# Two reorderings in the streaming part of a graph kernel: word numbers before the row sums on TensorE, raw scores before the copies of turned rows on ScalarE

## The reference

```python
h = relu(layernorm(x))
H = h @ W.T + b; s = H @ a_s; r = H @ a_r
e = leaky_relu(A * s + A * r.T, 0.2)
att = softmax(where(A > 0, e, -9e15), axis=1)
x = x + att @ H                          # layer 0: attention over the neighbours
h = relu(layernorm(x)) @ weight
out = relu(adj @ h + bias)
x = x + max over the neighbours of out   # layer 1: sum, then graph max-pool
```

## Time and profile before

| | us |
|---|---|
| median of 3 runs | 2826.6 |
| lowest and highest | 2820.92, 2831.66 |
| the profiled execution | 2835.18 |
| its span in the trace | 2826.0 |
| the stretch in which steps 18 to 76 run | about 280 to 1430 |

### The profile page before, as it was taken

The page is one execution under the profiler, slowest core; times in us unless marked ns, Lnnn a source line. Parts: engine busy times, 40 slices in busy tenths (PEclk is TensorE's granted clock), DMA queues, the critical chain, the costliest instruction groups (busy, mean ns, idle before and its releaser), DMA issues.

```text
span 2826.0 us, 19035 instructions
## 1 busy us (share of the span) xinstructions
PE 968.4 (34%) x4534; PEld 535.7 (19%) x4534; DVE 1438.5 (51%) x3301; ACT 456.3 (16%) x1519; POOL 1562.0 (55%) x1616
## 2 busy tenths in 40 slices
PE   3664156525245536423539996600000000000000
PEld 1431133213122213323514432300000000000000
DVE  6888677855334525443265543547656345222222
ACT  1631145302123214433410000000000000000000
POOL 0102755444664645576363564677766755677776
PEclk8987577767677768666759997855555555555555
DMA  9999668788567879632441221152232111222121
GB/s 351 410 381 375 189 239 291 283 224 321 194 241 244 297 261 387 212 79 70 120 97 40 75 61 48 51 132 59 67 56 43 52 42 40 48 57 54 49 47 41
DMA packets 155983, 447.42 MB, mean 158 GB/s; under 512 B 34557, under 2 KB 81459, under 8 KB 122970
## 3 DMA queue, kind: packets, MB, share of 16 engines
q1 hardware_dynamic: 80506, 311.94, 29.2%
q0 software_dynamic: 53184, 114.44, 16.9%
q10 hardware_dynamic: 22176, 19.77, 2.3%
HBM read 408.06 MB, written 37.95 MB: 158 GB/s over the span
## 4 chain that ended last, share of the span: by engine, by line
another core or an unknown queue 20%; POOL 18%; PE 16%; issue 15%; DVE 11%; DMA 6%; DVEq 6%; ACT 4%; SPq 2%; ACTq 1%; POOLq 0%
POOL ring L661 16%; PE psV L1093 9%; DMA a_buf<-in_adj 5%; PE psV L920 3%; DVE squares L1330 2%; SPq L390 2%; ACT ring L764 2%; POOL out L667 1%; PE psH L976 1%; DVE a_buf L1495 1%; DVEq L1499 1%; DVE words L1221 1%; DVE words L1212 1%; DVEq L1215 1%
## 5 line engine op out<-in xcount | busy, mean ns | idle before, releaser
L589 POOL DMA_INDIRECT ring<-h_table,srec x518 | 506.5, 978 | 304.0 <-issue 170.3
L661 POOL DMA_INDIRECT ring<-p_table,srec x545 | 529.8, 972 | 200.3 <-issue 166.9
L920 PE MATMUL psV<-a_buf,bit_ident 128*128 128x512 bf16 x1024 | 318.4, 476 | 245.7 <-DMA a_buf<-in_adj 173.8
L1330 DVE TENSOR_REDUCE squares<-ring 128x128 f32<-128x640 f32 (+15 forms) x99 | 178.0, 1798 | 333.4 <-DMA ring<-p_table,srec 301.9
L976 PE MATMUL psH<-ring,ident 128*128 128x128 f32 x1036 | 159.3, 316 | 205.9 <-remote 93.2
L624 POOL DMA_INDIRECT ring<-y_table,srec x198 | 191.8, 969 | 62.4 <-issue 61.8
L1093 PE MATMUL psV<-rec_all,a_buf 128*128 128x512 bf16 x888 | 202.0, 385 | 26.0 <-issue 25.9
L1103 PE MATMUL psH<-ones_row,flag_col 128*1 128x1 f32 x2 | 0.2, 163 | 589.7 <-DVEq L1556 589.7
L920 PEld LDWEIGHTS psV<-a_buf,bit_ident 128*128 128x128 bf16 x1024 | 115.5, 115 | 432.3 <-issue 296.0
L976 PEld LDWEIGHTS psH<-ring,ident 128*128 128x128 f32 x1036 | 149.6, 228 | 220.2 <-issue 205.9
L1314 DVE SCALAR_TENSOR_TENSOR e_sc<-e_sc 128x6 f32<-128x6 f32 (+19 forms) x63 | 10.7, 170 | 259.1 <-ACT e_sc L748 245.0
(11 more groups left out here) (228 smaller groups left out, 2055.5 us busy)
## 6 DMA issues: line engine op xcount, KB each, us to landing
a_buf<-in_adj SPq DMA_DIRECT2D x256, 1024.0 KB
ring<-p_table,srec POOLq DMA_INDIRECT x545
ring<-h_table,srec POOLq DMA_INDIRECT x518
trec<-records ACTq DMA_DIRECT2D x63, 128.5 KB
packed<-wbuf ACTq DMA_DIRECT2D x28, 256.0 KB
a_buf<-packed SPq DMA_DIRECT2D x7, 1024.0 KB
h_table<-stage POOLq DMA_DIRECT2D x16, 258.0 KB, 7.6
a_buf<-r_row SPq DMA_DIRECT2D x1, 4096.0 KB
```

What stands on the lines that cost most here:

```text
L589: pool.indirect_dma_start(ring[:, A_AT[q] + j, :], None, h_table, bass.IndirectOffsetOnAxis(srec_u[g][:, i, LIST + j:LIST + j + 1], 0)).th ...
L661: pool.indirect_dma_start(ring[:, C_AT[n] + j, 0:D], None, p_table, bass.IndirectOffsetOnAxis(slot, 0)).then_inc(s_rows[n % BUFS], 16)
L920: last = pe.matmul(psV[n % 2][:, h * BANK:(h + 1) * BANK].rearrange("p (g n) -> p g n", n=P), bit_ident[:, k, :], rows[:, :, k, :], start= ...
L1330: dve.tensor_reduce(to, ring[:, at:at + n, 0:D].rearrange("p s d -> p d s"), AX.X, op)
```

## The change

On ACT, `raw_scores` of a step moves from behind the record loads to a place ahead of `tile_copies`. On PE, `number_words(n+1)` moves from behind `turn_rows` to directly behind `pack(n+1)`. Nothing is added or removed.

```diff
@@ scalar engine, step n @@
                 if 1 <= n <= 8:
                     normalize(2 * n - 2)
                     normalize(2 * n - 1)
+                for q in AT_STEP[n]:
+                    raw_scores(q)
                 if n in TURNS:
                     tile_copies(n)
                 if n in DENSE_STEP:
@@
                 for q in AT_STEP[n + 1] if n < LAST else []:
                     load_record(q)
-                for q in AT_STEP[n]:
-                    raw_scores(q)
                 for q in AT_STEP[n]:
                     exponents(q)
@@ tensor engine, step n @@
                 if n + 1 < T:
                     pack(n + 1)
+                if n + 1 < T - 1:
+                    number_words(n + 1)
                 for q in AT_STEP[n - 1]:
                     sum_slots(q)
                 if n in TURNS:
                     turn_rows(n)
-                if n + 1 < T - 1:
-                    number_words(n + 1)
```

## The result

The changed kernel takes 2816.84 us (median of 8 runs, 2811.45 to 2820.77) against 2826.4 us for the kernel before (8 runs, 2820.92 to 2832.97): ratio 0.9957, 95% interval 0.9945 to 0.9970. The forecast was 2816.6 us. A second comparison gave 0.9942 (0.9919 to 0.9965), 2819.56 against 2834.88 us.

A forecast was written before the change was run, and what follows sets the result against it. PE's signals, held to the end of gather runs, were taken to bound steps 18 to 76. Terms -3.0, -4.4, -2.6 and 0 gave -10 us, from 2826.6 to 2816.6; own range 2811 to 2824, full range 2799 to 2836.

The forecast's parts named there:

- Late signals: Steps 18 to 76: engines that wait for PE late in a run of gathers wait to the run's end.
- rival C: ACT itself stands still, so raw scores delay each turn by 0.40 us a tile: +10 us, 2837; chance 0.16.
- Numbers, 0: Word numbers directly behind the pack gain 0; in dense steps, if not hidden, they cost up to 3 us.
- T: The moment PE's signals arrive; copy, scatter and next gathers form a loop from it, whose length the change leaves.
- Group 1, -3.0: Step 19: raw scores no longer stand behind `keep_words`, so scores and POOL's next gather come 3 us earlier.
- Group 2, -4.4: End of group 2: the last extraction comes at 897.4 instead of 901.89, so POOL's start at 921.94 gains 4.4 us.
- Group 3, -2.6: End of group 3: DVE scores near 1184.1 instead of 1186.66, and the scatter at 1195.99 gains 2.6 us.
- The T cycle of steps 55 to 62 stays: Group 3: the loop from PE's signals to the next keeps its length; +0.6 at 55 and 56, given back at 61.
- Steps 64 to 76, 0: Raw scores cost +2.6 us in steps 70 to 72, about -2.6 in 73 to 75: sum 0, ends -3 and +3.
- A: Only the turn's signal is late, so DVE isn't held at the close and runs ahead: -25 us, 2802; chance 0.24.
- B: The gain is absorbed by PE's longer dense steps and another wait in group 2: -2 to -4 us, 2823; chance 0.15.
- D: The change does nothing, DVE being busy whenever raw scores are ready; counted inside the forecast and the absorbed-gain rival.

The follow-up runs named there:

- e9: The changed kernel plus two useless activations on ACT, ahead of its wait for the turn: ratio 0.9937 to the kernel before.
- e8: The changed kernel, with POOL waiting ahead of every fourth gather until its last one has landed: ratio 1.0458 to the kernel before.
- e5: The kernel before, unchanged, profiled a second time: record scatters of groups 1 to 3 at 518.9, 926.0 and 1192.0 us.
- e7: The changed kernel, with the numbers left behind the turn where the next tile's packed words are kept: ratio 0.9922 to the kernel before.
- e12: The kernel before, with raw scores moved only in steps 64 and later, signals held: ratio 0.9964 to the kernel before.
- e11: The kernel before, with only the raw scores moved, in every step, signals held: ratio 0.9921 to the kernel before.
- e10: The changed kernel plus two useless activations on ACT, behind the wait for the turn and ahead of the copies: ratio 0.9956 to the kernel before.
- e1: The kernel before, with only the raw scores moved, in every step, measured where no signals were held: ratio 0.9982 to the kernel before.
- e3: The kernel before, with raw scores moved only in steps 64 and later, measured where no signals were held: ratio 0.9975 to the kernel before.

## Why the prediction was right, and where it wasn't

**Late signals (right, and too narrow).** All that hung on "PE's signals arrive at the end of a run" was seen: DVE and ACT released together (896.18, 896.21), ACT working in the hold (e9), the hold gone with the gapless run (e8). It has exceptions in the long runs. In the changed kernel one copy comes at 827.75, 16.8 us into a run of 25 gathers (811 to 842), for a turn that ended at 799.77. And the extraction of step 52, which started at 1020.87 in the kernel before, 6.6 us after POOL's last instruction, starts in the middle of a run (974 to 1008) in the changed one:

```profile
998.03 1.23 DVE L1212 MAX8 words<-psV 128x8 f32<-128x1024 f32 x1 [23.01 <-remote]
```

Nor is the prediction's border, 5 us into the run, sharp: all turns later than that were held, but so was one that ended 3.6 us into its run (copy at 1140.75, 9.4 us late). And it isn't only signals. Late in a long run PE and DVE get single instructions, with nothing to wait for, 1.4 us or a multiple of it apart. In e5:

```profile
356.03 0.37 PE L976 MATMUL psH<-ring,ident 128*128 128x128 f32 x1 [2.52 <-issue]
...
358.83 0.37 PE L977 MATMUL psH<-trec,ident 128*128 128x128 f32 x1 [2.43 <-issue]
...
361.63 0.37 PE L977 MATMUL psH<-trec,ident 128*128 128x128 f32 x1 [2.42 <-issue]
```

```profile
354.68 0.57 DVE L1237 SCALAR_TENSOR_TENSOR node<-node,label 128x320 f32<-128x320 f32 x1 [2.31 <-issue]
...
357.47 0.49 DVE L1240 MAX8 rec_all<-node 128x8 f32<-128x320 f32 x1 [2.21 <-issue]
...
361.67 0.50 DVE L1245 MAX8 rec_all<-node 128x8 f32<-128x320 f32 x1 [2.24 <-issue]
```

ACT is not spared in the first long run (280 to 360). In the kernel before:

```profile
335.41 0.40 ACT L764 ACTIVATE ring<-ring,prob 128x128 f32<-128x128 f32 x1 [0.98 <-issue]
336.80 0.40 ACT L767 ACTIVATE trec<-trec,prob 128x128 f32<-128x128 f32 x1 [0.99 <-issue]
338.19 1.02 ACT L721 ACTIVATE wbuf<-psV 128x1024 bf16<-128x1024 f32 x1 [1.00 <-issue]
```

So an engine that is itself slowed does occur, as rival C had it, but not at the copies that the forecast rests on. What makes these steps of 1.4 us the traces don't show; code that arrives late, which the prediction left open, is not excluded for them.

**Numbers, 0: mis-sized.** T in steps 21, 23 and 25 became PE's, as said: the copies at 404.27, 445.36 and 479.98 come 0.03, 1.15 and 0.03 us behind the turn's end. But the price, 3 to 4 us from step 20 to step 26, was not hidden, and no gain by the early numbers is seen anywhere. It doesn't show at the end of group 1 because the raw scores gained as much in the same steps (113.9 and 114.0 us in the kernel before, 109.9 in e7; 115.1 in e12 and 110.6 in e11, of one comparison), which the forecast had at nothing behind step 19. Two terms that were both put at nothing cancel.

**Group 1, -3.0.** Measured -3.5 (mean of two executions each). In the changed kernel all of it is step 19, as said: the extraction of step 20 starts 3.3 us earlier, and the lead stays to the end of the group (3.7 at the extraction of step 26).

**Group 2, -4.4.** The sum to here was -7.4; measured -7.2 on the means, -5.0 on the first pair. The right sum has a wrong composition. The term itself held: DVE's distance from the last T before the last extraction fell from 5.35 (4.60 in the second trace) to 0.7 us. That group 1's 3.0 would add to it was the failed step: e7, e9 and e10 show the run of gathers up to 856 swallowing such shifts. The rest of the -7.2 is T itself, at 896.5 and 901.0 in the two executions of before and 896.2 and 896.0 in the changed ones: one late execution of the kernel before, and so luck in the mean.

**Group 3, -2.6: mis-sized, measured -7.5 for its stretch.** The forecast's own term is not in it: from the extraction of step 62 to the scatter the kernel before takes 29.1 and 24.3 us and the changed one 26.2 twice, so -2.9 on the first pair and -0.5 on the means. Some 3.3 us come at step 52, where the first execution of the kernel before had its extraction held to 1020.87; the second took 120.9 us from step 46 to step 53, nearly what the changed kernel does (120.1, 120.2). That part is scatter. The remaining 3.9 us are the change's. "The T cycle of steps 55 to 62 stays" was the failed step. It stays from step 57 on. In steps 55 and 56 no hold covers the turn: PE packs late (in the kernel before its matmuls at 1072.92 waited 5.14 us for a tile's load), and sums and turn follow. There DVE's distance counts in full. Step 56 before, then changed:

```profile
1082.42 0.27 PE L998 MATMUL psT<-ident,hn 128*128 128x128 f32 x1
...
1085.10 0.17 DVE L1314 SCALAR_TENSOR_TENSOR e_sc<-e_sc 128x8 f32<-128x8 f32 x1 [7.44 <-ACT e_sc L748]
...
1087.40 1.23 DVE L1212 MAX8 words<-psV 128x8 f32<-128x1024 f32 x1
```

```profile
1072.10 0.27 PE L998 MATMUL psT<-ident,hn 128*128 128x128 f32 x1
...
1072.30 0.16 DVE L1337 RECIPROCAL l_inv<-l_sum 128x1 f32<-128x1 f32 x1 [1.40 <-PE psH L977]
...
1073.02 1.23 DVE L1212 MAX8 words<-psV 128x8 f32<-128x1024 f32 x1
```

From the turn to the extraction it was 4.98 us and is 0.92. Between the extractions of steps 53 and 57 the changed kernel takes 55.5 and 56.0 us instead of 59.5 and 59.8, and in the comparison of e11 and e12, which differ there by the raw scores alone, it is 55.6 against 60.5.

**Steps 64 to 76, 0: mis-sized, and its +0.85 in steps 70 to 72 had the wrong sign.** The third scatter to L624 takes 7.6 us less (means), alone (e12) 225.1 against 229 to 235. Of the 245.0 us of waits with which the prediction begins, 123.4, ten waits, lie in this stretch (window 1196 to 1431), and the forecast gave them nothing. It priced 0.85 us of raw scores ahead of L790 and didn't look at what stands behind the exponents. ACT from step 70 to the copy of step 71, before, then changed:

```profile
1351.04 0.36 ACT L803 ACTIVATE rec_all<-psT,t_rstd 128x128 f32<-128x128 f32 x1
...
1353.65 0.58 ACT L817 ACTIVATE hn<-psF 128x512 f32<-128x512 f32 x1
...
1363.11 0.60 ACT L817 ACTIVATE hT<-psF 128x512 f32<-128x512 f32 x1 [5.12 <-remote]
...
1366.90 0.42 ACT L790 ACTIVATE hT<-psT 128x128 f32<-128x128 f32 x2
```

```profile
1330.79 0.36 ACT L803 ACTIVATE rec_all<-psT,t_rstd 128x128 f32<-128x128 f32 x1
...
1332.03 0.57 ACT L817 ACTIVATE hn<-psF 128x512 f32<-128x512 f32 x1
...
1338.50 0.60 ACT L817 ACTIVATE hT<-psF 128x512 f32<-128x512 f32 x1 [2.98 <-PE psF L1016]
...
1344.55 0.45 ACT L790 ACTIVATE hT<-psT 128x128 f32<-128x128 f32 x2 [1.40 <-remote]
```

From L803 to the first L817 it was 2.61 us and is 1.24, because the raw scores and DVE's scores no longer lie between. The fourth L817 thus gets PE's signal 4.5 us into POOL's run (from 1334.01) and not too late (run from 1354.25). Held, it took both normalizations with it behind T: L790 came at T + 3.8. Now only L790 is held. A turn's cycle, L790 to L790, falls from 17.87 us (1349.03 to 1366.90) to 15.78 (1328.77 to 1344.55).

**The rivals.** A (DVE runs ahead) has fallen: DVE was held at the close, 76.3 us. B came in part: e7, e9 and e10 show group 1's gain absorbed, but the whole was not. C has fallen by e9. D, the change does nothing, is excluded by the interval, which ends at 0.9970.

**What the right number hides.** Up to L624 the traced gain is 22.3 us (means of two), more than twice the forecast's 10; the medians give 9.6 and 15.3. Part of the difference is the choice of executions (own times 17.6 us apart on average), the late T and the held step 52 of the kernel before among it. Another part may be the last stage, from L624 to the end of the span: 1395.0 and 1399.8 us before, 1399.2 and 1404.0 changed. Its work is unchanged; whether these 4 us are more than scatter (e7, e9 and e10: 1398.0, 1402.6, 1399.0) was not settled. So terms that were too small met something of the other sign, and that the median came within 0.3 us of 2816.6 is luck. The second comparison, with 15.3 us, is the fairer measure of how well the sum did. The ends of the forecast's own range don't follow from its terms either: added up at their ends they give 2812.8 to 2826.5, not 2811 to 2824.

## What to carry to other kernels

Work that doesn't need a late signal should stand ahead of the wait for it: moving two small instructions a tile gave 0.8% here (e11), nearly half of it in steps that held half of the waits read at the start and were priced at nothing. Look where in time a total of waits lies before deciding which steps to price. When pricing such a move, follow what stands behind the moved instruction as well as what it is put ahead of: 1.4 us less ahead of ACT's next work decided whether that work fell before or behind a hold. And a wait for a third engine (here for the copied words) must not come along with a move ahead of others' work; split the move by steps.

## What the runs showed of the hardware

During gapless gathers on POOL (one in 1.25 us) the other engines can be held: a signal of PE given more than about 5 us into a run, and some given from 2.6 us on, is in the short runs seen 1 to 3 us after the run's end (14 of 15 such copies in the changed kernel's trace; the fifteenth came inside a long run). In long runs it can be over 30 us late (986.31 to 1020.87), and single instructions of PE, DVE and ACT start only every 1.4 or 2.8 us. When POOL waits ahead of every fourth gather until the one before has landed, it is nearly gone (e8). With the same kernels (e1 is e11, e3 is e12) and the same spacing it doesn't happen at all in another comparison, where the kernel before takes 2492 us instead of 2830, on a chip with the same number in the record. The traces don't show why; a profile of one execution says nothing about how such a kernel runs elsewhere.
